# A new instruction order on four engines ahead of a selective scan, and one wait more at its end

## The chip, the cores and the metric

The kernel runs on one NeuronCore of one Trainium2 chip. The metric is the device time of one execution in microseconds (us). Three executions of the kernel before took 268.91, 266.67 and 266.70 us, median 266.7. The profile shown here comes from one further execution, which took 264.77 us; the span of its instructions is 263.0 us.

## The reference: what is computed

The input is one sequence of 2048 tokens with 128 channels, in fp32. Four layers follow each other, each of the form `x = layernorm(x + f(x))`:

1. attention over channels: 16 heads of 8 channels, scores summed over the tokens, so the softmax works on 8x8 blocks;
2. a gated feed-forward: `sigmoid(xr @ Wr) * (relu(xk @ Wk)**2 @ Wv)`, xr and xk mixing each token with the one before it;
3. the state layer, to which the change belongs;
4. a gated MLP with 512 hidden channels and three further products (silu, gelu, gelu).

Layer 3, cut to what matters:

```
lifted  = tanh(relu(x @ Wl1 + bl1) @ Wl2 + bl2)
x_trans = relu(concat(x, lifted) @ Wf1 + bf1) @ Wf2 + bf2
Bm, Cm  = x_trans @ W2 + b2, x_trans @ W3 + b3           # 16 states each
delta   = softplus(x_trans @ W1 + b1)
dA      = exp(-celu(delta[..., None] * A))
h_new   = dA * h_prev + x_trans[..., None] * (delta[..., None] * Bm[..., None, :])
out     = sum over states of Cm * h_new
```

h_prev is the same for all tokens, so no step depends on the token before. The kernel uses that the second part of h_new, summed over the states, is `x_trans * delta * sum(Bm * Cm)`; this is what is called the direct term below.

## The kernel before, in words

Activations are held transposed: 128 channels on the partitions, 2048 tokens along the free axis, cut into four chunks c = 0 to 3 of 512 tokens (`CH`, `NCH`). PSUM has eight banks of 512 fp32 columns; banks c and 4+c serve chunk c in turn. Each engine has a program of its own, written out by hand as a list of calls such as `fusion(2)` or `state_t(0)`; an engine carries out its list strictly in that order, and every call first waits on semaphores for its inputs. There is no planner: the position of a call in its engine's list is all that sets the order.

**Normalisation of layer 2 and the layers of layer 3.** TensorE makes the centred sum (`y2(c)`), ScalarE squares it (`square`, line 519), TensorE averages the squares (`y2_variance(c)`, L1135), ScalarE takes logarithm and exponential (`rstd_of`, L524 and L526), VectorE multiplies and splits into a high and a low part (`second_input(c)`, L879, L854, L856). Then, per chunk, TensorE and ScalarE go to and fro: `layer1`, `layer2` (tanh), `fusion_input` and `fusion` (relu), `transformed` (the product for x_trans on TensorE, L1193, and its bias on ScalarE, L561), `step_input` (L1198) and `c_and_b` (L1203). VectorE bounds the step size's input (`bounded`, L897), ScalarE takes exp and ln (`log_exp` L567, `log_ln` L573), VectorE finishes delta (`step_size`, L903); ScalarE copies C out of PSUM (`c_copy`, L617), VectorE multiplies C by B (`c_times_b`, L909), TensorE sums over the states and spreads the sum (`b_times_c`, L1208), VectorE multiplies x_trans by it (`weighted`, L915). `delta_copy` (L1256) puts delta back into PSUM for the scan. Between these, ScalarE and VectorE carry side work for later stages: `low_magnitude` (L513), `fill_low` (L816), and `state_weights` (L477), which writes 16 masked copies of the initial state, `h0sel`.

**The scan.** Token pairs of chunks (0,1) and (2,3) are taken one after the other, each in eight groups of two states; e = 0 to 15 counts the groups, and seven buffers (`vbuf`) hold them. For a group, `state_t(e)` on ScalarE (L630, two instructions) takes exp of delta times the negative part of A; `state_v(e)` on VectorE (L922) adds delta times the positive part, except for nine of the 32 states, where GpSimd does it with `z_product` (L395) and `v_sum` (L403); `state_da(e)` on ScalarE (L638) takes exp(1 - v); TensorE writes C times the initial state into banks 0 to 3 (`state_ch`, L1213), VectorE multiplies (`state_p`, L930 for the second state, L936 for the first); GpSimd adds the two states of a group in 13 of the first 15 groups (L424); and TensorE sums the groups in PSUM (`state_sum`, L1237). Banks 0 to 3 are the banks of `b_times_c`, so the first `state_ch` waits until `weighted` has run for all four chunks. GpSimd also rounds C and takes its low part (`c_parts`, L372 and L374) and multiplies the direct term by delta (`direct`, L382).

**After the scan** VectorE makes the input of layer 4 chunk by chunk (`x3(c)`: L950, the rounding to the high part L854, the low part L856), and TensorE starts the MLP with `gated` (L1346, L1347). DMAs lie at the start (inputs) and at the end (output) only; the change adds and moves none.

Of the kernel before, what the change touches and what calls it, by code (L numbers as in the profile page):

```python
# [31 lines left out]
NS = 16  # L32
# [12 lines left out]
def build(nc, t, out):  # L45
# [13 lines left out]
    with ctx:  # L59
# [3 lines left out]
        def sem(name):  # L63
            return ctx.enter_context(nc.semaphore(name))
# [56 lines left out]
        def sb_and_f32(name, width):  # L121
# [49 lines left out]
        h0f_ok, h0sel_ok, a_ok = [  # L171
            sem(n) for n in ("h0f_ok", "h0sel_ok", "a_ok")]
# [34 lines left out]
        def cs(c):  # L207
            return slice(c * CH, (c + 1) * CH)
# [123 lines left out]
        def _(pool):  # L332
# [36 lines left out]
            def c_parts(c):  # L369

                pool.wait_ge(c_full, c + 1)
                g.tensor_copy(tr[0:96, 0, cs(c)], bs3[0:96, cs(c)]).then_inc(c_hi, 1)  # L372
                pool.wait_ge(c_hi, c + 1)
                g.tensor_tensor(tr[32:64, 0, cs(c)], bs3[32:64, cs(c)], full(tr[32:64, 0, cs(c)]),  # L374
                                ALU.subtract).then_inc(c_lo, 1)
                pool.wait_ge(c_lo, c + 1)
# [29 lines left out]
            c_parts(1)  # L406
            c_parts(2)
            pool.wait_ge(a_ok, 2)
            z_product(0)
            v_sum(0)  # L410
            z_product(1)
            v_sum(1)
            pool.wait_ge(e_vp, 2)
            c_parts(3)
            r = 2
            for e in range(NE - 1):
                if r < len(on_pool) and on_pool[r][0] == e + 2:
                    z_product(r)
                    v_sum(r)
                    r += 1  # L420
                if e in POOL_ADDS:
                    pool.wait_ge(e_p, e + 1)
                    b = vbuf[e % NB]
                    g.tensor_tensor(b[:, 0, :], b[:, 0, :], b[:, 1, :], ALU.add).then_inc(e_add, 1)  # L424
                if 1 <= e <= 2:
                    direct(2 * e - 2)
                    direct(2 * e - 1)
# [15 lines left out]
        def _(act):  # L443
# [114 lines left out]
            def transformed(c):  # L558

                act.wait_ge(xt_mm, c + 1)  # L560
                a.activation(bxt[:, cs(c)], ps[:, c, :], ACT.Identity, bias=vec[:, BF2:BF2 + 1]).then_inc(xt_ok, 1)  # L561

# [34 lines left out]
            layer2(0)  # L597
            layer2(1)
            low_magnitude(2)
            fusion(0)  # L600
            layer1(2)
            fusion(1)
            layer1(3)
            transformed(0)
            state_weights(11, 13)
            layer2(2)
            transformed(1)
            state_weights(13, NS)
            layer2(3)
            fusion(2)  # L610
# [43 lines left out]

            log_exp(0)
            transformed(2)
            c_copy(0)
            low_magnitude(3)
            log_exp(1)
            fusion(3)  # L660
            log_ln(0)
            log_ln(1)
            c_copy(1)
            transformed(3)
            c_copy(2)
            act.wait_ge(a_ok, 2)
            state_t(0)
            state_t(1)
            c_copy(3)
            state_t(2)  # L670
# [52 lines left out]
        def _(dve):  # L723
# [125 lines left out]

            def split(full_sem, hi_sem, lo_sem, full_buf, dst, c):  # L850

                hi, lo = dst(c)
                dve.wait_ge(full_sem, c + 1)
                v.tensor_copy(hi, full_buf[:, cs(c)]).then_inc(hi_sem, 1)  # L854
                dve.wait_ge(hi_sem, c + 1)
                v.tensor_tensor(lo, full_buf[:, cs(c)], full(hi), ALU.subtract).then_inc(lo_sem, 1)  # L856


            for c in range(NCH):
                dve.wait_ge(y1_rs, c + 1)  # L860
                v.tensor_tensor(bx1[:, cs(c)], ps[:, 4 + c, :], bs2[:, cs(c)], ALU.mult).then_inc(x1_ok, 1)
                split(x1_ok, x1_hi, x1_lo, bx1, lambda c: parts(x1r, c, 2), c)
                if c == 0:
                    fill_low(5)

# [17 lines left out]
            fill_low(6)  # L883
            gate(1)
            fill_low(7)
            gate(2)
            gate(3)
            second_input(0)
            fill_low(8)
            second_input(1)  # L890
            second_input(2)
            second_input(3)

# [58 lines left out]

            bounded(0)
            fill_low(9)
            fill_low(10)
            bounded(1)
            c_times_b(0)
            weighted(0)
# [3 lines left out]
            c_times_b(2)  # L962
            dve.wait_ge(low_mm, 1)
            v.tensor_reduce(low_any[:, :], ps[:, FLAG_BANK, 0:NLOW], AX.X, ALU.add).then_inc(low_flag, 1)
# [3 lines left out]
            weighted(1)  # L968
            weighted(2)
            bounded(2)  # L970
            c_times_b(3)
            bounded(3)
            state_v(1)
            weighted(3)
# [111 lines left out]
        def _(pe):  # L1086
# [176 lines left out]
            rk(3)  # L1263
            value(1)
            y2(0)
            value(2)
            y2(1)
            y2_variance(0)
# [11 lines left out]
            fusion_input(1)  # L1280
            layer2(1)
            layer1(2)
            fusion(0)
            layer1(3)
            fusion(1)
            transformed(0)
            layer2(2)
            transformed(1)
            layer2(3)
            fusion_input(2)  # L1290
            fusion(2)
            step_input(0)
            c_and_b(0)
            transformed(2)
            fusion_input(3)
            step_input(1)
            c_and_b(1)
            fusion(3)
            b_times_c(0)
            transformed(3)  # L1300
            c_and_b(2)
            delta_copy(0)
# [3 lines left out]
            delta_copy(1)  # L1306
            b_times_c(1)
            step_input(2)
            c_and_b(3)
# [3 lines left out]
            pe.wait_ge(h0sel_ok, NS)  # L1313
# [195 lines left out]
```

## Time and profile before

| | us |
|---|---|
| three executions, median | 266.7 |
| profiled execution | 264.77 |
| span of its instructions | 263.0 |
| busy: TensorE / VectorE / ScalarE / GpSimd | 230.9 / 205.9 / 187.3 / 123.6 |
| normalisation of layer 2, layers of layer 3 | about 50 to 92 |
| scan | about 92 to 164 |
| MLP and output | about 162 to 263 |

Busy time is the union of an engine's instructions; TensorE's includes waits inside pipelined matmuls. No engine is busy all the time over the whole span, so an engine's total says little: each stage has to be read for what its last wait ends on.

### The profile page before, as it was taken

What the parts mean: (1) busy time and instruction counts of PE and PEld (TensorE: products, weight loads), DVE (VectorE), ACT (ScalarE), POOL (GpSimd) and SP (SyncE); (2) the same over time, 40 slices, a digit from 0 to 9 for tenths busy, and PEclk for the clock granted to TensorE, in tenths of its full rate; (3) what the DMA queues carried; (4) which work ended last, traced back from release to release, by engine and by line L of the source; (5) the groups of instructions that cost most, each with busy time, mean ns of one, the idle gap of its engine ahead of it and who ended that gap; (6) DMA issues with size and microseconds to landing.
All of it is one profiled execution on the core that took longest, in us unless ns stands there. A gap on an engine that the chain in (4) does not pass through costs nothing.

```text
span 263.0 us, 2685 instructions
## 1 busy us (share of the span) xinstructions
PE 230.9 (88%) x857; PEld 151.7 (58%) x857; DVE 205.9 (78%) x335; ACT 187.3 (71%) x258; POOL 123.6 (47%) x96
## 2 busy tenths in 40 slices
PE   6898899999999569978686997999999999999970
PEld 6896557545543134533242554568888678888850
DVE  4997792776059899975999999982499997997475
ACT  4489899979999999768998984359933643544330
POOL 3420000000026977999999984283244567065300
PEclk9799999999999855999997999999999999999995
DMA  5960000000000000000000000000000000110002
GB/s 131 373 247 1 1 0 2 0 0 0 0 0 0 0 5 0 1 0 4 0 0 1 0 0 0 2 0 0 0 0 2 0 0 0 44 40 1 0 0 80
DMA packets 4847, 6.16 MB, mean 23 GB/s; under 512 B 384, under 2 KB 2656, under 8 KB 4832
## 3 DMA queue, kind: packets, MB, share of 16 engines
q1 hardware_dynamic: 4832, 5.97, 6.8%
q8 instruction: 8, 0.13, 0.2%
q14 instruction: 7, 0.06, 0.1%
HBM read 4.92 MB, written 1.05 MB: 23 GB/s over the span
## 4 chain that ended last, share of the span: by engine, by line
PE 45%; DVE 27%; ACT 11%; issue 8%; POOL 5%; DMA 2%; SPq 0%; DVEq 0%; POOLq 0%; ACTq 0%
PE ps L1346 9%; PE ps L1347 8%; PE ps L1237 4%; PE ps L216 2%; DVE tr L1021 2%; PE ps L217 2%; PE ps L218 2%; DMA bx<-in_x_dram 2%; PE ps L1135 2%; POOL bxt L382 2%; POOL bs L403 2%; DVE bx L930 2%; PE ps L1213 2%; DVE bx L936 2%; DVE xr L1018 2%
## 5 line engine op out<-in xcount | busy, mean ns | idle before, releaser
L711 ACT ACTIVATE bs<-ps,vec 128x512 f32<-128x512 f32 x48 | 31.7, 690 | 36.8 <-PE ps L1347 34.4
L1213 PE MATMUL ps<-tr,h0sel 96*128 96x512 f32 x64 | 26.7, 532 | 10.5 <-DVE bx L930 3.1
L372 POOL CAST tr<-bs 96x512 fp32r<-96x512 f32 x4 | 2.4, 608 | 64.1 <-ACT bs L617 63.9
L1213 PEld LDWEIGHTS ps<-tr,h0sel 96*128 96x128 f32 x64 | 12.6, 213 | 23.4 <-issue 13.1
L1346 PE MATMUL ps<-xr,wf 128*128 128x512 f32 x64 | 25.4, 396 | 0.0
L1347 PE MATMUL ps<-xr,wf 128*128 128x512 f32 x64 | 25.3, 396 | 0.0
L438 POOL TENSOR_TENSOR xr<-bs,xr 128x512 fp32r<-128x512 f32 x12 | 16.1, 1350 | 17.4 <-DVE xr L1018 17.4
L438 POOL TENSOR_TENSOR tr<-bs,tr 128x512 fp32r<-128x512 f32 x8 | 10.9, 1359 | 23.0 <-DVE tr L1018 23.0
L438 POOL TENSOR_TENSOR x1r<-bs,x1r 128x512 fp32r<-128x512 f32 x12 | 13.8, 1153 | 8.5 <-DVE x1r L1018 8.5
L1018 DVE CAST tr<-bs 128x512 fp32r<-128x512 f32 x16 | 7.4, 487 | 12.9 <-ACT bs L711 12.9
L1346 PE MATMUL ps<-lr,wf 128*128 128x512 f32 x32 | 14.4, 450 | 2.4 <-DVE lr L856 1.5
L1237 PE MATMUL ps<-bx,centre 128*128 128x512 f32 x28 | 15.8, 700 | 0.0
L1347 PE MATMUL ps<-x1r,wf 128*128 128x512 f32 x40 | 15.7, 393 | 0.0
L1346 PE MATMUL ps<-x1r,wf 128*128 128x512 f32 x40 | 15.7, 392 | 0.0
L1347 PE MATMUL ps<-tr,wf 128*128 128x512 f32 x40 | 15.7, 391 | 0.0
L1346 PE MATMUL ps<-tr,wf 128*128 128x512 f32 x40 | 15.7, 391 | 0.0
L638 ACT ACTIVATE bs<-bs 128x2048 f32<-128x2048 f32 x6 | 11.4, 1906 | 5.7 <-POOL bs L403 5.7
L424 POOL TENSOR_TENSOR bs<-bs 128x1024 f32<-128x1024 f32 x6 | 14.3, 2381 | 2.2 <-DVE bs L936 2.2
L922 DVE SCALAR_TENSOR_TENSOR bx<-ps,amax,bx 128x1024 f32<-128x1024 f32 x11 | 13.6, 1275 | 0.1
L1347 PEld LDWEIGHTS ps<-xr,wf 128*128 128x128 f32 x64 | 12.0, 188 | 2.9
L1346 PEld LDWEIGHTS ps<-xr,wf 128*128 128x128 f32 x64 | 12.0, 188 | 2.8
L630 ACT ACTIVATE bs<-bdl,amin 128x1024 f32<-128x1024 f32 x12 | 13.1, 1142 | 0.0
(229 smaller groups left out, 687.0 us busy)
## 6 DMA issues: line engine op xcount, KB each, us to landing
wf_raw<-in_w_mlp_dram SPq DMA_DIRECT2D x2, 1024.0 KB, 9.3
bx<-in_x_dram SPq DMA_DIRECT2D x4, 256.0 KB, 6.2
out_dram<-bdl SPq DMA_DIRECT2D x4, 256.0 KB, 2.3
wf_raw<-in_w_mlp_dram SPq DMA_DIRECT2D x1, 768.0 KB, 11.8
bdl<-in_w_ssm_dram SPq DMA_DIRECT2D x1, 448.0 KB, 8.8
wa<-in_w_attn_dram SPq DMA_DIRECT2D x1, 256.0 KB, 2.8
w0raw<-in_w_ffn_dram SPq DMA_DIRECT2D x1, 192.0 KB, 8.3
h0T<-in_state_dram SPq DMA_DIRECT2D x1, 48.0 KB, 6.2
```

Source lines behind the costliest of these rows:

```text
L216: nc.tensor.matmul(dst, w[0], xs[0], start=start, stop=False)
L424: g.tensor_tensor(b[:, 0, :], b[:, 0, :], b[:, 1, :], ALU.add).then_inc(e_add, 1)
L438: g.tensor_tensor(sl[:, 1, o, :], hbuf[k][:, o, :], full(sl[:, 0, o, :]), ALU.subtract).then_inc(m_lo_p, 1)
L630: a.activation(vbuf[e % NB][:, j, :], bdl[:, pair_tokens(e)], ACT.Exp, scale=amin[:, n:n + 1]).then_inc(e_t, 1)
L638: a.activation(vbuf[e % NB][:, :, :], vbuf[e % NB][:, :, :], ACT.Exp, scale=-1.0, bias=1.0).then_inc(e_da, 1)
L711: a.activation(hbuf[k][:, o, :], ring(mbank(i, stage, k, o)), ACT.Gelu if stage else ACT.Silu, scale=vec[:, s + o:s + o + 1]).then_inc(m_a ...
L922: v.scalar_tensor_tensor(tile, delta_ps, amax[:, n:n + 1], tile, ALU.mult, ALU.add).then_inc(e_v, 1)
L1018: v.tensor_copy(sl[:, 0, o, :], hbuf[k][:, o, :]).then_inc(m_hi, 1)
L1213: last = m.matmul(ps[:, 2 * j + k, :], h0sel[:, group_states(e)[j], :], tr[0:96, 0, cs(2 * (e // NG) + k)], start=True, stop=True)
L1237: last = m.matmul(ps[:, SUM_BANK + k, :], centre[:, :], vbuf[e % NB][:, j, k * CH:(k + 1) * CH], start=(e % NG == 0 and j == 0), stop=(e % ...
L1346: m.matmul(dst, wf[:, f, 0, wo], x[0], start=start, stop=False)
L1347: last = m.matmul(dst, wf[:, f, 0, wo], x[1], start=False, stop=stop and not low_weights)
```

## The change

No operation is dropped or added in the arithmetic. Three of its parts move work between engines or places in a stage, one adds a wait:

- the four `transformed(c)` biases go from ScalarE to VectorE, as do five of the 16 `state_weights` (numbers 11 to 15), with a semaphore of their own;
- the lists of TensorE, ScalarE and VectorE are reordered from the normalisation of layer 2 to the scan's group 3. On TensorE `y2(0)` comes ahead of `value(1)`, and `y2(1)` behind `y2_variance(0)`. In the state layer chunks 0 and 1 now go through to their step sizes before chunks 2 and 3 are taken past `layer2`, and ScalarE has `state_t(0)`, `state_t(1)` and `state_t(2)` among the `fusion` and `c_copy` of chunks 2 and 3;
- on GpSimd the four `direct(c)` go from the scan's iterations 1 and 2 to a place ahead of the loop (0 and 1) and to iterations 0 and 1 (2 and 3), among the `c_parts`;
- before its last addition (e = 14) GpSimd waits for the low part of `x3(0)`.

```diff
@@ gpsimd @@
             c_parts(0)
-            c_parts(1)
-            c_parts(2)
             pool.wait_ge(a_ok, 2)
             z_product(0)
+            direct(0)
+            pool.wait_ge(o2_ok, 1)
+            c_parts(1)
             v_sum(0)
             z_product(1)
+            pool.wait_ge(e_zp, 2)
+            c_parts(2)
+            direct(1)
+            pool.wait_ge(o2_ok, 2)
+            c_parts(3)
             v_sum(1)
-            pool.wait_ge(e_vp, 2)
-            c_parts(3)
             r = 2
             for e in range(NE - 1):
...
                 if e in POOL_ADDS:
                     pool.wait_ge(e_p, e + 1)
+                    if e == NE - 2:
+                        pool.wait_ge(x3_lo, 1)
...
-                if 1 <= e <= 2:
-                    direct(2 * e - 2)
-                    direct(2 * e - 1)
+                if e == 0:
+                    direct(2)
+                if e == 1:
+                    direct(3)
@@ scalar @@
             layer2(0)
+            layer1(2)
+            low_magnitude(2)
             layer2(1)
-            low_magnitude(2)
+            layer1(3)
             fusion(0)
-            layer1(2)
+            layer2(2)
             fusion(1)
-            layer1(3)
-            transformed(0)
-            state_weights(11, 13)
-            layer2(2)
-            transformed(1)
-            state_weights(13, NS)
             layer2(3)
-            fusion(2)
             act.preload_act_table_set(LN_EXP)
...
+            low_magnitude(3)
             log_exp(0)
-            transformed(2)
             c_copy(0)
-            low_magnitude(3)
+            log_ln(0)
             log_exp(1)
-            fusion(3)
-            log_ln(0)
             log_ln(1)
             c_copy(1)
-            transformed(3)
-            c_copy(2)
             act.wait_ge(a_ok, 2)
             state_t(0)
+            fusion(2)
             state_t(1)
+            fusion(3)
+            state_t(2)
+            c_copy(2)
             c_copy(3)
-            state_t(2)
             state_da(0)
             log_exp(2, 2)
             state_t(3)
@@ vector @@
+            def state_weights(n0, n1):
+                for n in range(n0, n1):
+                    v.tensor_scalar(h0sel[:, n, :], h0T[:, :], one_state[:, n:n + 1], None, ALU.mult).then_inc(h0sel_dve, 1)
...
+            def transformed(c):
+                dve.wait_ge(xt_mm, c + 1)
+                v.tensor_scalar(bxt[:, cs(c)], ps[:, c, :], vec[:, BF2:BF2 + 1], None, ALU.add).then_inc(xt_ok, 1)
...
             gate(0)
             fill_low(6)
+            fill_low(7)
             gate(1)
-            fill_low(7)
             gate(2)
+            fill_low(8)
             gate(3)
             second_input(0)
-            fill_low(8)
             second_input(1)
             second_input(2)
             second_input(3)
+            fill_low(9)
+            fill_low(10)
+            state_weights(12, NS)
...
+            transformed(0)
+            transformed(1)
             bounded(0)
-            fill_low(9)
-            fill_low(10)
             bounded(1)
             c_times_b(0)
-            weighted(0)
             step_size(0)
             step_size(1)
             c_times_b(1)
-            c_times_b(2)
-            dve.wait_ge(low_mm, 1)
-            v.tensor_reduce(low_any[:, :], ps[:, FLAG_BANK, 0:NLOW], AX.X, ALU.add).then_inc(low_flag, 1)
+            weighted(0)
             state_v(0)
             weighted(1)
+            transformed(2)
+            transformed(3)
+            state_v(1)
+            c_times_b(2)
+            c_times_b(3)
+            dve.wait_ge(low_mm, 1)
+            v.tensor_reduce(low_any[:, :], ps[:, FLAG_BANK, 0:NLOW], AX.X, ALU.add).then_inc(low_flag, 1)
+            bounded(2)
             weighted(2)
-            bounded(2)
-            c_times_b(3)
+            weighted(3)
             bounded(3)
-            state_v(1)
-            weighted(3)
             state_v(2)
             state_p(0)
@@ tensor @@
             rk(3)
+            y2(0)
             value(1)
-            y2(0)
             value(2)
+            y2_variance(0)
             y2(1)
-            y2_variance(0)
             value(3)
...
             fusion_input(1)
+            layer1(2)
             layer2(1)
-            layer1(2)
             fusion(0)
             layer1(3)
+            layer2(2)
             fusion(1)
             transformed(0)
-            layer2(2)
+            layer2(3)
             transformed(1)
-            layer2(3)
-            fusion_input(2)
-            fusion(2)
             step_input(0)
             c_and_b(0)
+            step_input(1)
+            fusion_input(2)
+            c_and_b(1)
+            b_times_c(0)
+            delta_copy(0)
+            delta_copy(1)
+            fusion_input(3)
+            fusion(2)
+            fusion(3)
+            b_times_c(1)
             transformed(2)
-            fusion_input(3)
-            step_input(1)
-            c_and_b(1)
-            fusion(3)
-            b_times_c(0)
             transformed(3)
             c_and_b(2)
-            delta_copy(0)
+            c_and_b(3)
             pe.wait_ge(low_ok, NLOW)
             pe.wait_ge(w_ok, 1)
             m.matmul(ps[:, FLAG_BANK, 0:NLOW], ones[:, :], low_max[:, :], start=True, stop=True).then_inc(low_mm, 1)
-            delta_copy(1)
-            b_times_c(1)
             step_input(2)
-            c_and_b(3)
             b_times_c(2)
             step_input(3)
             b_times_c(3)
-            pe.wait_ge(h0sel_ok, NS)
+            pe.wait_ge(h0sel_ok, 11)
+            pe.wait_ge(h0sel_dve, NS - 11)
```

## Rows read from the trace of the kernel before

**Rows 1.** Stretches: span, its length, each engine's busy us (count), clock share, DMA.
```profile
60.00:80.00 20.00, 20.00 (x55) 10.16 (x56) 7.75 (x14) 19.16 (x33) 1.87 (x2) 1.00 0.00 0
110.00:120.00 10.00, 8.26 (x25) 4.23 (x23) 6.85 (x6) 4.62 (x5) 9.83 (x6) 1.00 0.01 2
```

**Rows 2.** Chain in order of time, 84 to 128: start, us, what.
```profile
107.38 2.53 POOL bxt L382 x2
111.09 2.36 POOL bs L403
```

**Rows 3.** Waits, 86 to 126: who for whom, total us, times, longest.
```profile
ACT bs L638 <- POOL bs L403: 5.4, 2, 3.5
```

**Rows 4.** Timeline of GpSimd: start, us, instruction, count, idle time before and its releaser.
```profile
105.03 2.39 POOL L424 TENSOR_TENSOR bs<-bs 128x1024 f32<-128x1024 f32 x1 [1.31 <-DVE bs L936]
...
119.29 2.35 POOL L424 TENSOR_TENSOR x1r_f<-x1r_f 128x1024 f32<-128x1024 f32 x1
```

**Rows 5.** Timeline of TensorE around the normalisation of layer 2.
```profile
50.95 1.08 PE L1135 MATMUL ps<-bs,centre 128*128 128x512 f32 x2
52.41 1.12 PE L1135 MATMUL ps<-bs,ones 128*128 128x512 f32 x2 [0.38 <-ACT bs L519]
```

**Rows 6.** Timeline of ScalarE in the same stretch.
```profile
51.76 1.08 ACT L519 ACTIVATE bs<-ps 128x512 f32<-128x512 f32 x2
53.58 0.69 ACT L524 ACTIVATE bs<-ps,eps_ln 128x512 f32<-128x512 f32 x1 [0.73 <-PE ps L1135]
61.60 0.69 ACT L546 ACTIVATE bs<-ps,vec 128x512 f32<-128x512 f32 x1 [0.50 <-PE ps L218]
```

**Rows 7.** Timeline of ScalarE, 70 to 92.
```profile
74.86 0.69 ACT L561 ACTIVATE bxt<-ps,vec 128x512 f32<-128x512 f32 x1
81.67 4.25 ACT L630 ACTIVATE bx<-bdl,amin 128x1024 f32<-128x1024 f32 x4
90.45 1.04 ACT L567 ACTIVATE bs<-bs 128x1024 f32<-128x1024 f32 x1
```

**Rows 8.** Timeline of VectorE, 73 to 123.
```profile
73.14 0.75 DVE L897 TENSOR_SCALAR bs<-ps,vec 128x512 f32<-128x512 f32 x1 [9.54 <-PE ps L1198]
...
79.78 1.40 DVE L903 SCALAR_TENSOR_TENSOR bdl<-ps,vec,bs 128x512 f32<-128x512 f32 x2
...
93.19 1.22 DVE L930 TENSOR_TENSOR bx<-bx,ps 128x1024 f32<-128x1024 f32 x1 [0.25 <-PE ps L1213]
...
102.61 1.21 DVE L930 TENSOR_TENSOR bs<-bs,ps 128x1024 f32<-128x1024 f32 x1
...
121.37 1.22 DVE L930 TENSOR_TENSOR bs<-bs,ps 128x1024 f32<-128x1024 f32 x1 [3.53 <-ACT bs L638]
```

**Rows 9.** Timeline of TensorE, 73 to 92.
```profile
73.80 1.02 PE L1193 MATMUL ps<-bs,bdl 128*128 128x512 f32 x2
...
89.23 1.12 PE L1208 MATMUL ps<-lr_f,ones_n 32*128 32x512 f32 x2 [1.17 <-DVE lr_f L909]
91.89 2.04 PE L1213 MATMUL ps<-tr,h0sel 96*128 96x512 f32 x4 [1.54 <-DVE bxt L915]
```

**Rows 10.** Timeline of GpSimd and VectorE at the scan's end.
```profile
157.99 2.73 POOL L424 TENSOR_TENSOR bx<-bx 128x1024 f32<-128x1024 f32 x1 [0.47 <-DVE bx L936]
...
158.54 2.45 DVE L854 CAST lr<-bxt 128x512 fp32r<-128x512 f32 x1
...
165.88 0.43 DVE L854 CAST lr<-bxt 128x512 fp32r<-128x512 f32 x1
```

**Rows 11.** Timeline of TensorE at the scan's end.
```profile
161.87 0.47 PE L1346 MATMUL ps<-lr,wf 128*128 128x512 f32 x1 [1.46 <-DVE lr L856]
...
166.78 1.88 PE L1237 MATMUL ps<-bx,centre 128*128 128x512 f32 x4
```

**Rows 12.** Stretches as in rows 1, for the granted clock (third value from the end).
```profile
90.00:91.00 1.00, 0.35 (x1) 0.00 (x0) 1.00 (x1) 1.00 (x2) 1.00 (x1) 0.65 0.00 0
...
103.00:104.00 1.00, 1.00 (x4) 0.40 (x2) 1.00 (x2) 1.00 (x2) 0.72 (x1) 0.53 0.00 0
```

More of the change, by code:

```diff
@@ L170, in build @@
             sem(n) for n in ("mu1_ok", "w0f_ok", "w0_hi", "w0_lo", "w1_hi", "w1_lo")]
-        h0f_ok, h0sel_ok, a_ok = [
-            sem(n) for n in ("h0f_ok", "h0sel_ok", "a_ok")]
+        h0f_ok, h0sel_ok, h0sel_dve, a_ok = [
+            sem(n) for n in ("h0f_ok", "h0sel_ok", "h0sel_dve", "a_ok")]
         fill_hi0, fill_hi, fill_lo, state_mask = [
@@ L556, in fusion @@
                 a.activation(bs1[:, cs(c)], ps[:, 4 + c, :], ACT.Relu, bias=vec[:, BF1:BF1 + 1]).then_inc(f1_ok, 1)
-            def transformed(c):
-                act.wait_ge(xt_mm, c + 1)
-                a.activation(bxt[:, cs(c)], ps[:, c, :], ACT.Identity, bias=vec[:, BF2:BF2 + 1]).then_inc(xt_ok, 1)
             def log_exp(c, count=1):
@@ L863, in _ @@
                 if c == 0:
+                    state_weights(11, 12)
+                if c == 1:
                     fill_low(5)
+            def transformed(c):
+                dve.wait_ge(xt_mm, c + 1)
+                v.tensor_scalar(bxt[:, cs(c)], ps[:, c, :], vec[:, BF2:BF2 + 1], None, ALU.add).then_inc(xt_ok, 1)
             def gate(c):
```

## The prediction, made before the changed kernel was run

> **What bounds the kernel now.** I read the busy shares by stretch first, then the chain of waits from 44 to 163 us, then each engine's timeline where the change acts. In the layers of the state layer TensorE is busy for the whole of 60 to 80 us, while ScalarE has 0.84 us to spare and VectorE is idle for 60% of the stretch; between 110 and 120 us the picture is another one, GpSimd is busy 9.83 of 10 us and VectorE and ScalarE wait [rows 1]. The chain of waits says the same: from 105 to 119.4 us it runs over GpSimd, through `direct(2)` and `direct(3)` at 107.38 and then `v_sum` for group 5 [rows 2]. ScalarE waits 5.4 us in two pieces for `v_sum` [rows 3], and VectorE 3.5 us for ScalarE behind it, until 121.37 [rows 8]. GpSimd's last free time before that is 1.31 us ahead of the addition of group 2 at 105.03, and from there to the end of `v_sum` for group 6 at 119.29 it has none [rows 4]. From 121.37 VectorE sets the pace until `x3(0)`. So a microsecond taken off GpSimd's list between 105 and 119 is worth one; one taken off ScalarE in the layers is worth one only if TensorE can use it.
>
> **The normalisation of layer 2.** Costed at a small loss. `y2_variance(0)` starts at 52.41, 0.65 us after the first square, which itself sits behind a table load; `y2(1)` ran ahead of it, at 50.95 [rows 5]. Now `y2(1)` stands behind it: that product spans 1.12 with 0.15 of overlap, so `y2(1)` starts at 53.38, and its square about 1.1 later (the Ln at 53.58 answers the product at 52.41 in 1.17), at 54.45 and not at 52.3 [rows 5, 6]. ScalarE takes its calls in order, so the first Ln goes from 53.58 to about 54.95. It had waited 0.73 there already [rows 6]. Followed op by op with today's durations (0.57 a step of ScalarE, 0.70 for Ln, 0.86 a product), ScalarE reaches the second `layer1` at 62.4, against 61.60 [rows 6], where it used to have 0.50 of waiting to give: **0.8 us late**. `y2(0)` ahead of `value(1)` puts VectorE's gate 0.86 later, and `fill_low(7)` fills the hole.
>
> **The layers, first half.** TensorE has eleven products from behind the second `layer1` to `transformed(1)`, eight of 0.86 (a product of two passes spans 1.02, of which 0.16 overlaps the next) and three of three passes at 0.70: 62.2 + 9.0 = 71.2 [rows 9]. The bias on ScalarE costs 0.69 with the overlap in it [rows 7]; on VectorE I take the 0.75 of `bounded`, which has the same source bank, size and operation [rows 8]. It is idle there for 9.54 us [rows 8], so the moved `fill_low`s and the four late `state_weights` cost nothing: for these no row shows the shape on VectorE, I bound one by 0 and 0.75, and five are at most 3.75, less than that idle time. If that cover were gone, `transformed(0)` would be late by as much. The two step sizes then need the ScalarE chain from the table load's end (72.6): `low_magnitude(3)` 1.6, two exps, two logs and a copy, to 77.1; `step_size(1)` ends at 77.85. Today both end at 81.2 [rows 8]. So `state_t(0)` starts at about 78.0, against 81.67 [rows 7]: **3.7 us early**, for the first two groups.
>
> **The layers, second half, gives it back.** The scan's first product needs `weighted` of all four chunks, since they share banks 0 to 3. Chunks 2 and 3 now hang on `fusion(2)` and `fusion(3)`, which ScalarE does behind exps of 1.06 each, four in 4.25 [rows 7]. From 78.0: 2.1 for `state_t(0)`, `fusion(2)` when TensorE delivers at 80.75, 2.1 for `state_t(1)`, `fusion(3)` to 84.1. TensorE's `transformed(3)` ends at 85.05, VectorE's bias at 86.0, `c_and_b(3)` at 86.95; then come `step_input(2)`, `b_times_c(2)`, `step_input(3)`, `b_times_c(3)` to 91.1 (1.05 each for the last kind, from 89.23 on [rows 9]) and `weighted(3)` to 91.9. The first `state_ch` starts at 92.0, against 91.89 [rows 9]. In total TensorE's work is the same, and its list was already full; it had 1.17 and 1.54 us of waiting ahead of the two last entries [rows 9], and now has about as much spread over the half behind it. What ScalarE sheds (four biases at a pitch of 0.57, 2.3 us, and five small copies) buys nothing here.
>
> **A new wait.** `bounded(3)` now stands behind `weighted(3)`, and ScalarE's `log_exp(2, 2)` waits for it until 92.6; it started at 90.45 [rows 7]. Behind it on ScalarE queue `state_t(3)`, `log_ln`, `state_da(1)`, and for that waits VectorE's `state_p(1)`. VectorE had not been waiting there, so of 2.1 only a part shows: `state_p(0)` at 93.8, against 93.19; `state_p(2)` at 103.2, against 102.61 [rows 8]: **+0.6 us** at the place where GpSimd takes over. The 0.8 from the normalisation is in it. Bounds: -0.9 (the chains meet better; then GpSimd, 1.3 us ahead of its addition of group 2 by my count, would soon bind) and +2.1 (the wait shows in full).
>
> **GpSimd.** `direct` of all four chunks is done, by my count, at 104.3, in time that lies free today; `c_parts` and `v_sum` for groups 1 to 3 still end before ScalarE asks (`v_sum` of group 2 at 94.6, needed at about 100). The addition of group 2 starts at 105.6 instead of 105.03, and `direct(2)`, `direct(3)`, 2.53 us [rows 2], no longer stand behind it: `v_sum` for group 6 ends at 105.6 + 14.26 - 2.5 = 117.4, against 119.29, where the next addition starts [rows 4]. ScalarE is free by 116.8 and VectorE by 117.7, so both take the whole of it: `state_p(6)` at 119.5, against 121.37 [rows 8]. **-2.5 us**, net of the lag **-1.9**. From there the lists are those of today and move as a block.
>
> **The wait at the end.** The last addition of GpSimd runs from 157.99 to 160.72, and VectorE's rounding in `x3(0)`, at 158.54, takes 2.45 us, where the same instruction at 165.88 with GpSimd idle takes 0.43 [rows 10]. It ended when the addition did. TensorE stood still 1.46 us for its result [rows 11]. With the wait the addition starts when `x3_lo` has landed. Rounding 0.43 instead of 2.45: **-2.0 us**. TensorE is by then still in its sum until 160.25 on today's clock, so its first product gains 1.6 and the later ones, which wait for `state_p(15)`, the full 2.0. Queued behind the waiting addition on GpSimd is only the MLP's work, which comes after that sum; who needs the addition is the sum at 166.78 [rows 11], on today's clock 164.8 now; it ends at 159.7 + 2.4 = 162.1, which leaves 2.7 us. The bounds are 0 (the rounding is slow for another reason) and 2.0.
>
> The final addition of VectorE, with both inputs in SBUF, would begin when GpSimd's has 0.1 us to go. The trace has no such overlap. The Trainium skill (SBUF — State Buffer, on the shared port pair) says such a pair of instructions excludes each other for a whole instruction; by that it would come 0.1 us later, and the sum above would be 3.8 in place of 3.9, with nobody waiting for it.
>
> **Sum.** -1.9 - 2.0 = -3.9 us. The profiled execution would go from 264.77 to 260.9. It lay 1.9 us under the median of the three runs, so I take the difference off the median: 266.7 - 3.9 = **262.8 us**.
>
> **Rivals.** A measurement of this kernel can tell about 1%, 2.7 us, from no change: the bounds are 264.0 and 269.4.
> - *My forecast*, 50%: 262.8, between 261.5 and 264.3, nearly all of it faster by over 1%.
> - *The front gains* (18%): if chunks 2 and 3 come through without `fusion` waiting behind the exps, the lag of 0.6 becomes a lead of up to 0.9, and GpSimd's free time is used up: 262.8 - 1.5 = 261.3. For it: ScalarE sheds 2.3 us and more. Against it: TensorE without a gap from 60 to 80 [rows 1].
> - *The new ScalarE wait eats GpSimd's gain* (17%): `log_exp(2, 2)` shows its whole 2.1 us in the scan, 0.4 is left of 2.5, with the 2.0 at the end: 264.3. For it: the exps from 81.67 on and this call stand on one engine, back to back [rows 7]. Against it: VectorE is the later of the two at `state_p(1)`.
> - *The end does not gain* (8%): the rounding stays slow, or the addition now meets something else: 264.8.
> - *Slower* (7%): TensorE falls to half clock in the layers. The granted clock falls to half, 1.2 GHz, at about 90.3 (a mean of 0.65 over that microsecond) and is back at 103.9 [rows 12], after TensorE had waited 1.17 and then again 1.54 us with one product between [rows 9]. Today this costs next to nothing, VectorE waits 0.25 [rows 8]. The new order has waits of 1.1 us before 52.4, and of about 0.7 before 76.2 and 84.2. If one tips the clock while TensorE's list is full, 13.6 us at half clock cost 6.8: 262.8 + 6.8 = 269.6. It decides from 6.6 us of loss on. Against it: between 110 and 120 TensorE was idle for 1.74 us and the clock stayed at 1.00 [rows 1].
>
> The Trainium skill (TensorE: Matmul & The Clock Gate, "What's actually happening") holds that the clock is halved by default and freed by sustained activity; by it a list with scattered short waits, as the new one, keeps its clock, which is why this rival gets no more.
>
> **Range and chances.** 260.6 to 265.7 takes in the forecast, both neighbouring rivals and the end without gain, with 0.8 us on either side for the scatter of the median (two of three runs within 0.03 us, one 2.2 above), and leaves out the slow case and the edges. Faster by over 1%: 0.46 + 0.17 + 0.02 = 0.65; slower: 0.05; the rest 0.30.
>
> **What would show it.** After the change: ScalarE's first Ln near 54.9; the two first step sizes done near 78 and `state_t(0)` right behind; the first `state_ch` within 1 us of 91.9; ScalarE idle before `log_exp(2, 2)`; `state_p(6)` near 119.5, with hardly any wait of ScalarE for `v_sum`; `x3(0)`'s rounding at 0.43 and TensorE without a hole ahead of the MLP. I am wrong if the first `state_ch` is off by more than 2 us, if VectorE still waits over 2 us before group 6, or if the clock is low between 60 and 90.

## The result, and the profile after

| | before | after |
|---|---|---|
| median, four executions each | 267.46 us | 263.6 us (262.92 to 264.32) |
| ratio of the times | | 0.9893, 95% interval 0.9847 to 0.9939 |
| the same on another chip, beside the experiments | 265.91 us | 262.94 us, ratio 0.9856 (0.9795 to 0.9916) |
| profiled execution (span) | 264.77 (263.0) us | 263.28 (261.5) us |

The change makes the kernel faster, by 1.1% (0.6 to 1.5%) in the first comparison and 1.4% in the second. The prediction was 262.8 us, 3.9 less than before. The two medians here differ by 3.9 us, while the ratio is worth 2.9 us (1.6 to 4.1). The two profiled executions differ by 1.5 us only, so the profiles have to say where 3.9 and 1.5 part.

The stretches of rows 1 first (columns as there: span, length, busy us of TensorE, its weight loads, VectorE, ScalarE, GpSimd; then granted clock, DMA):

```profile
60.00:80.00 20.00, 19.09 (x53) 9.42 (x52) 13.02 (x23) 18.06 (x27) 3.16 (x4) 1.00 0.00 0
90.00:91.00 1.00, 1.00 (x3) 0.24 (x3) 0.68 (x2) 0.17 (x1) 1.00 (x1) 1.00 0.00 0
110.00:120.00 10.00, 9.60 (x30) 5.05 (x28) 7.93 (x7) 8.53 (x7) 9.92 (x5) 1.00 0.01 2
130.00:140.00 10.00, 7.63 (x19) 3.59 (x17) 8.60 (x8) 8.91 (x9) 9.83 (x6) 0.88 0.00 1
```

TensorE is no longer busy all the time from 60 to 80, a first sign that the front has lost something. Between 110 and 120 ScalarE does 8.53 us of work where it did 4.62 [rows 1]. At 90 to 91 the clock is still whole (0.65 in rows 12). And there is something new: the clock of 130 to 140 is 0.88, and it was 1.00 in the profile of before. ScalarE's timeline after the change answers to rows 6 and 7:

```profile
50.75 1.28 ACT L587 ACT_TABLE_LOAD   x1
...
54.72 0.60 ACT L526 ACTIVATE bs<-ps 128x512 f32<-128x512 f32 x1 [2.07 <-PE ps L1148]
55.21 0.68 ACT L531 ACTIVATE bs<-ps,eps_ln 128x512 f32<-128x512 f32 x1
...
62.74 0.69 ACT L553 ACTIVATE bs<-ps,vec 128x512 f32<-128x512 f32 x1 [0.50 <-PE ps L218]
...
78.27 2.19 ACT L627 ACTIVATE bx<-bdl,amin 128x1024 f32<-128x1024 f32 x2 [0.31 <-DVE bdl L914]
...
93.37 1.06 ACT L569 ACTIVATE bs<-bs 128x1024 f32<-128x1024 f32 x1 [3.20 <-DVE bs L908]
```

The reader sees both new waits, 2.07 us for `y2(1)` and 3.20 us for `bounded(3)`, and the first pair of exps at 78.27. The first Ln, at 55.21, is the one forecast near 54.9. VectorE, with its calls as in rows 8 and the rounding of rows 10:

```profile
94.38 1.21 DVE L941 TENSOR_TENSOR bx<-bx,ps 128x1024 f32<-128x1024 f32 x1
...
103.94 1.21 DVE L941 TENSOR_TENSOR bs<-bs,ps 128x1024 f32<-128x1024 f32 x1
...
120.26 1.22 DVE L941 TENSOR_TENSOR bs<-bs,ps 128x1024 f32<-128x1024 f32 x1 [2.18 <-ACT bs L635]
...
134.49 1.22 DVE L941 TENSOR_TENSOR bs<-bs,ps 128x1024 f32<-128x1024 f32 x1 [1.40 <-PE ps L1226]
...
159.10 0.43 DVE L855 CAST lr<-bxt 128x512 fp32r<-128x512 f32 x1
```

`state_p(2)` starts later than before (103.94 against 102.61), `state_p(6)` earlier (120.26 against 121.37 [rows 8]), and the rounding in `x3(0)` takes 0.43 us. But it starts at 159.10, later than the 158.54 of rows 10: between group 6 and the end of the scan the lead was lost again, 1.40 us of it in one wait for TensorE at group 9. GpSimd, where rows 2 and 4 were:

```profile
103.56 1.28 POOL L382 TENSOR_TENSOR bxt<-bxt,bdl 128x512 f32<-128x512 f32 x1
106.36 2.38 POOL L430 TENSOR_TENSOR bs<-bs 128x1024 f32<-128x1024 f32 x1 [1.51 <-DVE bs L947]
108.71 1.13 POOL L395 TENSOR_SCALAR tr_f<-bdl,amax 128x1024 f32<-128x1024 f32 x1
...
118.19 2.37 POOL L430 TENSOR_TENSOR x1r_f<-x1r_f 128x1024 f32<-128x1024 f32 x1
...
160.40 2.40 POOL L430 TENSOR_TENSOR bx<-bx 128x1024 f32<-128x1024 f32 x1 [2.49 <-DVE lr L857]
```

The last direct term is done before the addition of group 2, and `z_product` follows that addition at once. From the addition's start to the end of `v_sum` for group 6 (where the next addition starts) it is 11.83 us, and it was 14.26 [rows 4]: 2.43 less. TensorE, for rows 9 and 11:

```profile
84.55 1.12 PE L1206 MATMUL ps<-bs,bdl 128*128 128x512 f32 x2 [0.46 <-ACT bs L563]
...
90.76 1.12 PE L1221 MATMUL ps<-lr_f,ones_n 32*128 32x512 f32 x2
92.76 1.17 PE L1226 MATMUL ps<-tr,h0sel 96*128 96x512 f32 x4 [0.87 <-DVE bxt L926]
...
160.40 0.79 PE L1360 MATMUL ps<-lr,wf 128*128 128x512 f32 x1
```

There is no hole any more ahead of the MLP's first product. Both executions can be laid over each other from the start of the table load ahead of the normalisation (50.47 before, 50.75 after; what lies ahead differs by 0.28 us). All times in this table are from that start, in us:

| | before | after | gained |
|---|---|---|---|
| first `state_ch` | 41.42 | 42.01 | -0.59 |
| `state_p(2)` | 52.14 | 53.19 | -1.05 |
| `state_p(6)` | 70.90 | 69.51 | +1.39 |
| rounding in `x3(0)` starts | 108.07 | 108.35 | -0.28 |
| MLP's first product | 111.40 | 109.65 | +1.75 |
| end of the span | 212.53 | 210.75 | +1.78 |

Read by the steps: the front costs 1.05, GpSimd gives 2.44, the scan's second half takes 1.67, the end gives 2.03. This compares one execution of each kernel; the experiments show which of these terms repeat.

### The profile page after: what moved, and what is told of

It is laid out like the page before. It is cut to its first block, busy times and chain, and to the rows that moved or that the text cites. A ratio compares the mean times of both kernels' runs of the same rounds, so it can differ in the third digit from the quotient of the medians.

```text
span 261.5 us, 2686 instructions
## 1 busy us (share of the span) xinstructions
PE 231.7 (89%) x857; PEld 152.4 (58%) x857; DVE 208.8 (80%) x344; ACT 183.6 (70%) x249; POOL 123.2 (47%) x96
## 3 DMA queue, kind: packets, MB, share of 16 engines
HBM read 4.92 MB, written 1.05 MB: 23 GB/s over the span
## 4 chain that ended last, share of the span: by engine, by line
PE 42%; DVE 23%; ACT 16%; POOL 10%; issue 7%; DMA 1%; DVEq 0%; POOLq 0%; ACTq 0%
PE ps L1360 8%; PE ps L1361 8%; PE ps L1250 7%; POOL bs L403 3%; PE ps L1148 2%; PE ps L1226 2%; PE ps L1133 2%; DVE tr L1034 2%; ACT lr_f L520 2%; POOL tr_f L395 2%; DVE xr L1031 2%; POOL bxt L382 1%; DVE tr L1031 1%; PE ps L216 1%; PE ps L1191 1%
## 5 line engine op out<-in xcount | busy, mean ns | idle before, releaser
L1226 PE MATMUL ps<-tr,h0sel 96*128 96x512 f32 x64 | 25.6, 512 | 11.7 <-DVE bx L941 3.8
L1226 PEld LDWEIGHTS ps<-tr,h0sel 96*128 96x128 f32 x64 | 12.0, 205 | 24.4 <-issue 12.1
L627 ACT ACTIVATE bx<-bdl,amin 128x1024 f32<-128x1024 f32 x12 | 13.1, 1136 | 0.3 <-DVE bdl L914 0.3
```

The costliest lines, as they stand in the source:

```text
L627: a.activation(vbuf[e % NB][:, j, :], bdl[:, pair_tokens(e)], ACT.Exp, scale=amin[:, n:n + 1]).then_inc(e_t, 1)
L1226: last = m.matmul(ps[:, 2 * j + k, :], h0sel[:, group_states(e)[j], :], tr[0:96, 0, cs(2 * (e // NG) + k)], start=True, stop=True)
```

## The experiments

Each kernel was timed in five rounds beside the kernel before on the same chip; there were three groups of four, each on a chip of its own. "Changed kernel" is the one of the diff.

**The wait at the end, alone.** Kernel before, and:

```diff
                     pool.wait_ge(e_p, e + 1)
+                    if e == NE - 2:
+                        pool.wait_ge(x3_lo, 1)
```

> The kernel before with the one new wait of GpSimd alone (its last addition after x3(0)'s low part). Theory: the rounding in x3(0) takes 0.43 us and not 2.45, TensorE has no hole ahead of the MLP, and the time falls by 2.0 us (ratio about 0.9925). Rival (the rounding is slow for another reason): no change. Rival (the late addition holds up TensorE's sum): slower by up to 1 us.

Measured: 264.46 us, ratio 0.9923 (0.9888 to 0.9959). VectorE:

```profile
159.49 0.43 DVE L856 CAST lr<-bxt 128x512 fp32r<-128x512 f32 x1
```

The MLP's first product follows this start after 1.3 us, and in the kernel before after 3.3. The step is worth its 2.0 us by itself, and nothing behind it is held up: from that product to the end of the span it is 101.1 us in both.

This profile shows one thing more. Up to the last addition of GpSimd, behind 158 us, this kernel's program is that of the kernel before, and the time from `state_p(6)` to the rounding should be the same. It is 38.15 us against 37.17. The clock has a stretch of half clock from 128.7 to 132.1 that the profile of before does not have, and VectorE waits for TensorE ahead of `state_p(9)`, as in the changed kernel:

```profile
129.00:130.00 1.00, 1.00 (x3) 0.42 (x2) 1.00 (x2) 1.00 (x2) 1.00 (x2) 0.50 0.00 0
...
135.09 1.22 DVE L932 TENSOR_TENSOR bs<-bs,ps 128x1024 f32<-128x1024 f32 x1 [0.91 <-PE ps L1215]
```

So the old order can have this loss too, and a profile of one execution does not say how often.

**The direct terms, alone.** Kernel before, and:

```diff
             c_parts(3)
+            direct(0)
             r = 2
...
-                if 1 <= e <= 2:
-                    direct(2 * e - 2)
-                    direct(2 * e - 1)
+                if e == 0:
+                    direct(1)
+                if e == 1:
+                    direct(2)
+                    direct(3)
```

> The kernel before with only GpSimd's four direct terms moved: direct(0) ahead of the loop, direct(1) in iteration 0, direct(2) and direct(3) in iteration 1, in GpSimd's free time ahead of the addition of group 2. Theory: v_sum of group 6 ends 2.5 us earlier, state_p(6) starts at about 118.9 instead of 121.4, and unless TensorE's half clock falls into the scan's second half, the time falls by 2.5 us (ratio 0.991). Rival (ScalarE or VectorE binds right behind GpSimd): state_p(6) gains under 1 us, ratio above 0.997.

Measured: 263.4 us, ratio 0.9894 (0.9836 to 0.9952). From the table load `state_p(6)` starts at 68.43 (before: 70.90), a gain of 2.47 us:

```profile
119.18 1.22 DVE L933 TENSOR_TENSOR bs<-bs,ps 128x1024 f32<-128x1024 f32 x1 [1.64 <-ACT bs L641]
...
156.83 2.46 DVE L857 CAST lr<-bxt 128x512 fp32r<-128x512 f32 x1
```

The slow rounding is still there, as it should be. Of the 2.47 us, 1.99 are left where the rounding starts: from `state_p(6)` to there it took 37.65 us against 37.17, with half clock from 136.6 to 143.5, where the profile of before has it from 141.5 to 144.9.

**Both of GpSimd's edits, without the new order of the other engines.**

> The kernel before with both of GpSimd's edits (as in the two kernels above), and the old order on TensorE, ScalarE and VectorE. Theory: minus 4.5 us (ratio 0.983), about 1 us faster than the changed kernel, because the new order of the other engines costs 0.6 to 1.3 us. Rival (the new order ahead of the scan gains by itself or makes the room for GpSimd's gain): slower than the changed kernel, ratio above 0.988.

Measured: 261.7 us, ratio 0.9826 (0.9768 to 0.9883). The two gains add up, and this kernel has the changed kernel's gain and 0.8 us more, though the intervals of the two ratios overlap. In its profile `state_p(2)` starts at 52.17 from the table load, as before the change, and not at 53.19. The new order is not needed for GpSimd's gain. It also has no stretch of half clock around 129: from `state_p(6)` to the rounding it took 37.25 us.

**The changed kernel again.**

> The changed kernel, unchanged, beside the others on the same chip. Ratio to before 0.985 to 0.990. The first state_ch at 92.8 and state_p(6) at 120.3; the stretches of half clock move a little from run to run.

Measured: 262.94 us, ratio 0.9856 (0.9795 to 0.9916). From the table load: first `state_ch` 41.99, `state_p(2)` 53.17, `state_p(6)` 69.49, rounding 108.23. Each is within 0.12 us of the first profile, the wait at group 9 included (1.31 us).

**The direct terms put back into the changed kernel**, in iterations 1 and 2, with `c_parts` as they were changed.

> The changed kernel with GpSimd's four direct terms back in iterations 1 and 2 of the scan. Theory: v_sum of group 6 and state_p(6) come 2.5 us later, and the ratio to before goes from 0.9856 to 0.995. Rival (in the new order ScalarE or VectorE binds, and the directs matter less than in the old): under 1.5 us later, ratio under 0.991.

Measured: 266.08 us, ratio 0.9969 (0.9934 to 1.0004). `state_p(2)` stays at 53.20, `state_p(6)` goes to 71.94, 2.43 us later:

```profile
122.61 1.22 DVE L936 TENSOR_TENSOR bs<-bs,ps 128x1024 f32<-128x1024 f32 x1 [3.50 <-ACT bs L630]
```

This is the wait of before (3.53). Without this step the rest of the change is worth 0.3%, not clear of zero.

**The old order in the normalisation**, in the changed kernel:

```diff
             rk(3)
-            y2(0)
             value(1)
+            y2(0)
             value(2)
-            y2_variance(0)
             y2(1)
+            y2_variance(0)
             value(3)
```

> The changed kernel with TensorE's old order in the normalisation of layer 2 (y2(1) ahead of y2_variance(0), y2(0) behind value(1)). Theory: ScalarE no longer waits 2.1 us for y2(1), its first Ln comes 1.3 us earlier, the table load before layer2(0) starts about 0.9 us earlier, and all that follows moves with it: minus 0.9 us against the changed kernel (ratio to before about 0.982). Rival (TensorE's full list in the layers swallows it): the first state_ch moves by less than 0.3 us, ratio unchanged at about 0.9856.

Measured: 262.09 us, ratio 0.9799 (0.9753 to 0.9844). ScalarE's wait of 2.07 us is gone:

```profile
50.65 1.28 ACT L587 ACT_TABLE_LOAD   x1
...
53.76 0.69 ACT L531 ACTIVATE bs<-ps,eps_ln 128x512 f32<-128x512 f32 x1 [0.73 <-PE ps L1148]
...
62.48 1.28 ACT L598 ACT_TABLE_LOAD   x1
```

The next table load comes 11.83 us behind the first; in the changed kernel it was 12.69. `state_ch`, `state_p(2)` and `state_p(6)` are all 0.84 to 0.86 us earlier. TensorE's list does not swallow it. The ratio alone would not show it, as its interval overlaps that of the changed kernel (0.9795 to 0.9916). In this profile half clock, from 128.7 to 132.1 and again from 139.0 to 145.8, took most of the gain back: 39.5 us from `state_p(6)` to the rounding, against 38.8.

**`bounded(3)` ahead of `weighted(3)`**, in the changed kernel:

```diff
             weighted(2)
+            bounded(3)
             weighted(3)
-            bounded(3)
             state_v(2)
```

> The changed kernel with VectorE's bounded(3) ahead of weighted(3), not behind it. Theory: bounded(3) fits into VectorE's wait of 1.25 us for the product of weighted(3), ScalarE's log_exp(2, 2) starts about 1.7 us earlier and its wait falls from 3.2 to 1.5 us, VectorE starts state_p(0) 0.66 us earlier relative to the first state_ch, and the scan moves by 0.6 to 0.7 us: ratio about 0.983. Rival (ScalarE's wait shows in full): minus 1.7 us, ratio 0.979. Rival (neither binds): no change.

Measured: 262.4 us, ratio 0.9826 (0.9779 to 0.9873). ScalarE waits 1.55 us instead of 3.20:

```profile
92.06 1.06 ACT L569 ACTIVATE bs<-bs 128x1024 f32<-128x1024 f32 x1 [1.55 <-DVE bs L908]
```

The first `state_ch` stays (42.02), `state_p(2)` starts 0.79 us earlier (52.40) and `state_p(6)` 0.78 (68.73). Of ScalarE's 1.65 us half reaches the path, since VectorE is the later of the two; the 0.64 that VectorE itself saves shows at `state_p(0)` already (42.99 against 43.63). Here too the intervals of the ratios overlap, and the gain is shown by the profile.

**The biases moved to VectorE, alone.** Kernel before, with `transformed(0)` and `(1)` ahead of `bounded(0)` on VectorE, `(2)` ahead of `bounded(1)`, `(3)` behind `weighted(0)`, and none on ScalarE:

```diff
+            def transformed(c):
+                dve.wait_ge(xt_mm, c + 1)
+                v.tensor_scalar(bxt[:, cs(c)], ps[:, c, :], vec[:, BF2:BF2 + 1], None, ALU.add).then_inc(xt_ok, 1)
```

> The kernel before with only the four biases of transformed moved from ScalarE to VectorE, otherwise the old order. Theory: TensorE's list is full from 60 to 88 us, so what ScalarE sheds buys nothing, and the time stays within 0.5 us of before (ratio 0.998 to 1.002). Rival (ScalarE's load mattered): minus 1 us or more, ratio under 0.9965. Rival (VectorE is now late for its own calls): plus 0.6 us or more.

Measured: 267.33 us, ratio 0.9998 (0.9965 to 1.0032): no gain from ScalarE's relief. In the profile even a loss, `state_p(0)` starts 43.69 us behind the table load (before: 42.72), and TensorE waits for a step size, which it did not before:

```profile
81.99 1.12 PE L1256 MATMUL ps<-bdl,ident 128*128 128x512 f32 x2 [0.65 <-DVE bdl L899]
```

**Zero products in TensorE's gap.** Changed kernel, with a tile `zeros` set to zero at the start, and at the end of an iteration of the scan:

```diff
+                    if e == 6:
+                        for k in (0, 1):
+                            m.matmul(ps[:, SUM_BANK + k, :], zeros[:, :], bxt[:, cs(0)], start=False, stop=False)
```

> The changed kernel with two more products per execution, of 0.86 us each, zeros times a stable tile, added into the two sum banks at the end of TensorE's iteration 6 of the scan, where it waits 2.2 us for VectorE. They change no value. Theory: the stretch of half clock from 129 to 132.4 us hangs on that wait; with it filled the clock stays at 1.00 there, VectorE's wait of 1.40 us for TensorE at 134.5 goes, and the time falls by 1.3 us (ratio about 0.981). Rival (that stretch has nothing to do with the wait): the half clock stays, and the products cost 0 to 0.4 us.

Measured: 261.86 us, ratio 0.9819 (0.9771 to 0.9867). The stretches of half clock in the second half, first of the changed kernel:

```profile
128.00:129.00 1.00, 0.67 (x3) 0.46 (x3) 1.00 (x2) 1.00 (x2) 1.00 (x2) 0.97 0.00 0
129.00:130.00 1.00, 1.00 (x3) 0.73 (x3) 1.00 (x2) 1.00 (x3) 1.00 (x1) 0.50 0.02 8
...
132.00:133.00 1.00, 1.00 (x3) 0.35 (x3) 1.00 (x1) 1.00 (x2) 0.92 (x2) 0.82 0.00 0
```

With the zero products the clock is 1.00 in every microsecond from 107 to 140, and TensorE's wait ahead of group 8 is 0.51 us where it was 2.23:

```profile
127.56 0.70 PE L1228 MATMUL ps<-tr,h0sel 96*128 96x512 f32 x2 [0.51 <-DVE bx L943]
```

From `state_p(6)` to the rounding it takes 37.1 us; it took 38.8 in the changed kernel and 37.2 in the kernel before. VectorE's wait for TensorE at group 9 is gone. In the profile that is the 1.7 us. That the products did it is not shown: the profile of before had the same wait of TensorE unfilled (2.24 us, ahead of 128.57) and kept its clock, that of the wait at the end alone had it too and did not. The medians do not decide it either: ratio 0.9819 here and 0.9856 for the changed kernel, with overlapping intervals.

**The two mends together** (old order in the normalisation, `bounded(3)` ahead).

> The changed kernel with two of its reorderings mended: TensorE's old order in the normalisation of layer 2, and VectorE's bounded(3) ahead of weighted(3). Each alone moved state_p(6) by 0.8 us. Theory: they add up, state_p(6) comes 1.6 us earlier than in the changed kernel, counted from the table load before the normalisation (67.9 us behind it, against 69.5), and the ratio to before is 0.980 (from 0.9856). Rival (GpSimd, 1.5 us ahead before the addition of group 2, binds): state_p(6) gains 0.8 to 1.0 us, ratio 0.982.

Measured: **260.58 us, ratio 0.9773** (0.9734 to 0.9813), the lowest ratio of all; its interval still touches that of the changed kernel (0.9795 to 0.9916). In the profile the two gains add up: `state_p(6)` starts 67.88 us behind the table load, 1.63 less than in the changed kernel, and GpSimd still waits 1.42 us ahead of the addition of group 2:

```profile
104.58 2.39 POOL L430 TENSOR_TENSOR bs<-bs 128x1024 f32<-128x1024 f32 x1 [1.42 <-DVE bs L947]
```

**The same with the zero products.**

> The same with the two zero products at the end of TensorE's iteration 6. Theory: the half clock around 129 us goes, VectorE does not wait for TensorE at group 8, minus 1.3 us more: ratio 0.975. Rival (the stretch of half clock only moves to another place where it costs as much): ratio as without them, 0.980.

Measured: 261.39 us, ratio 0.9808 (0.9762 to 0.9854); its interval overlaps the last one's, so nothing is gained. (The wait meant is the one of `state_p(9)`.) In the profile of the mended kernel without them the clock stayed up around 129 anyway, and was low from 138.8 to 142.2; with them it was low for twice as long, from 136.7 to 143.6 (this row has its start):

```profile
136.00:137.00 1.00, 0.00 (x0) 0.00 (x0) 1.00 (x2) 1.00 (x2) 0.92 (x2) 0.87 0.00 0
```

and from `state_p(6)` to the rounding it took 38.0 us, against 37.3. The time came out as the rival said, but there was no stretch around 129 for the products to remove, so neither the theory nor the rival's move to another place is tested. The mean clock of the six executions was even higher with them (median 0.9555 against 0.947), and the time was not shorter.

**GpSimd's two edits and the zero products, old order.**

> The kernel before with GpSimd's two edits and the two zero products, old order on TensorE, ScalarE and VectorE. Theory: it gains 0 to 1.3 us on the same kernel without the zero products (ratio 0.978 to 0.9826), and is slower than the mended changed kernel with them by about 0.5 us, which is what the new order is worth once its two faults are mended. Rival (the new order is worth nothing even mended): equal to it or faster.

Measured: 261.31 us, ratio 0.9803 (0.9761 to 0.9845), against 0.9826 without them, and 0.9808 for the mended kernel with them. No difference can be told. In the profiles, where the time up to `state_p(6)` repeats within 0.1 us, the mended new order is worth 0.58 us there (67.88 against 68.46).

## Why the prediction came out, point by point

**The wait at the end: right.** 2.0 was forecast, 2.03 in the profile, ratio 0.9923 when tried alone. The addition of GpSimd was needed 2.5 us after its end; 2.7 was forecast. For the MLP's first product I had reckoned 1.6, as the sum was still running; it gained the full 2.03.

**GpSimd's direct terms: right.** 2.5 was forecast; the profiles give 2.44 in the changed kernel, 2.47 in the kernel before and 2.43 taken out again. The rival in which the new wait of ScalarE eats this gain did not come: `state_p(2)` to `state_p(6)` lasts 16.3 us with the move in either order of the other engines (16.32 and 16.29), and 18.76 before.

**The normalisation: right.** 0.8 us late was forecast; it is 0.86 at the second `layer1`, and undoing it gives 0.84 to 0.86 everywhere behind. The price came from one row: the product at 52.41 and who would now stand behind it.

**The layers: right in kind.** The exps of the first group were forecast 3.7 us early, at 78.0, and started 27.52 us behind the table load, which is 78.0 on the clock of before. That all of it is given back was right too: the first `state_ch` was forecast 0.1 late and came 0.59 late. The term that was too small is TensorE's list between `transformed(3)` and `b_times_c(3)`: I took 6.9 us from its start, it lasted 7.3, as the products next to those of 32 rows have a pitch of about 1.05 and not 0.86 (84.55 to 91.88 above holds seven products and the small one).

**The new wait of ScalarE: underpriced.** 0.6 us at `state_p(2)` was forecast, of all front terms together, and 1.05 came. ScalarE waited 3.20 us, and putting `bounded(3)` back gives 0.79. Both of the front's faults are now shown by experiment, and together, 1.64 us, they are more than the whole lag: without both, the new order is 0.59 ahead at `state_p(2)` (51.55 against 52.14).

**Moving the biases buys nothing: right** in time (ratio 0.9998), though I had called it free for VectorE, and in the old order its profile shows 0.97 us of delay.

**What the sum left out: the second half of the scan.** "From there the lists are those of today and move as a block" is the step that failed. It put the granted clock at no cost. The lists did move, but TensorE's clock did not move with them: a further stretch of half clock, from 129.0 to 132.4, stood where `state_first(1)`, a sum and the next `state_ch` lie in a row on the path, and cost 1.67 us. Both profiles of the changed kernel have it. It is no mark of the new order, though: the profile with the wait at the end alone, whose order there is that of before, has it too and lost 0.98 us by it, and the profile of before, from which I worked, happens to be without it. In all fourteen profiles the time from `state_p(6)` to the rounding goes with the half clock between 116 and 150 us:

| half clock, 116 to 150 us | from `state_p(6)` to the rounding | profiles |
|---|---|---|
| one stretch of 3.4 us | 37.13 to 37.36 us | 5, before among them |
| one of 6.8 us | 37.65 and 37.96 us | 2 |
| two of 3.4 us, one near 129 | 38.15 to 38.84 us | 4, changed kernel among them |
| 10.2 us and more | 39.32 to 39.48 us | 3 |

Whether the new order makes the second stretch likelier is open. I had the half clock as a rival in the layers only, where the clock stayed at 1.00. I had also misread its example from before the change: the clock fell at 90.3 [rows 12], when the wait of 1.54 us (90.35 to 91.89 [rows 9]) was only beginning, so just the wait of 1.17 us lay ahead of it. That a list with scattered short waits keeps its clock held in the layers, and not in the scan.

With these terms the profiled execution comes out as it did: 1.05 - 2.44 + 1.67 - 2.03 = -1.75 us, and 0.28 us lost ahead of all this makes -1.5.

**The median came out at the forecast, 3.9 us, with 0.45 us and 1.67 us of loss that the forecast did not have.** The ratio's interval is wide enough, 0.61 to 1.53%, to hold 2 us and 3.9. One part can be named: the profiled execution of before, with a mean clock of 0.951 and 264.77 us, was better than the middle of its kind. The 17 executions of before beside the first group of experiments lie between 264.82 us at a clock of 0.957 and 269.71 us at 0.934, so such losses are common in the kernel before too, and a change that removes none of them is judged against executions that already have them. How much of the changed kernel's loss is usual and not of one execution, the medians do not tell. So the mechanism was right in GpSimd's term and the end's, 4.5 us together; that the two losses beyond the forecast, 2.1 us in the profile, left the medians' difference at 3.9 is in part luck.

## What to carry to other kernels

Where several engines work through fixed lists, price a reordering by the place where it is late, not by how early its first part is: here two groups of exps 3.7 us ahead were worth nothing, as the scan opens only when the last chunk is through. Look for work of an engine that is bound later (GpSimd at 105 to 119 us) that could run in its idle time now; that, and one wait that kept a GpSimd instruction off VectorE's rounding, were the whole gain, and neither needed the reordering they came with. Before a loss in one profile is put down to a change, look for it in a second execution of the old program: here the wait at the end alone served as one. When a reordering is made, look at each call that now stands behind a longer wait than it needs: the two found here were worth 1.6 us together.

## What the runs showed of the hardware

**GpSimd can hold up VectorE's rounding until its own instruction ends.** A cast of 128x512 from SBUF to SBUF takes 0.43 us alone and 2.45 beside a GpSimd addition that ran from 157.99 to 160.72 [rows 10]; in the three kernels without the wait it took 2.45 or 2.46, in all the others 0.43. VectorE's products with a PSUM operand took 1.21 to 1.22 us with GpSimd at work or not. The Trainium skill (SBUF — State Buffer, on the shared port pair) describes this as an exclusive lock for a whole instruction, and the trace agrees. It says the same of a VectorE instruction with two SBUF inputs beside a GpSimd one that reads SBUF. Two cases here bear on it, and the trace agrees in kind. The prediction says that the trace has no such overlap, but the kernel before has one: the first product of `x3(0)`, with both inputs in SBUF, ran when GpSimd's addition began at 157.99, and that addition took 2.73 us [rows 10] where GpSimd's other additions took 2.35 to 2.40; it was 2.73 and 2.72 in the two other kernels without the wait.

```profile
157.82 0.68 DVE L950 TENSOR_TENSOR bxt<-bxt,bdl 128x512 f32<-128x512 f32 x1
```

After the change VectorE's last addition started 0.25 us ahead of the end of GpSimd's and took 1.33 us, where it had taken 1.23, the 0.1 of the prediction:

```profile
162.55 1.33 DVE L1009 TENSOR_TENSOR bx<-bx 128x1024 f32<-128x1024 f32 x1
```

**The granted clock is a part of the time that no list shows.** In the 17 executions named above, time and mean clock have a correlation of -0.93; a mean clock lower by 0.01 goes with 1.7 us. In the middle of the scan each stretch of half clock began near the end of a wait of TensorE of 1.75 to 2.8 us, at most 1.3 us before it or 2.2 behind it, but not each such wait has one. The same program shows both: a wait of 2.24 us ahead of 128.57 without it in the kernel before, and one of 2.24 ahead of 128.54 with it in the kernel with the wait at the end alone. That filling such a gap keeps the clock up is not shown.
